# A fused attention, graph-convolution and LSTM block: ScalarE's reads and TensorE's products in a new order within each group of the first pass

## The chip, the cores and the metric

The kernel runs on one core of a Trainium2 chip. Five engines work side by side, each on its own queue in the order in which the program lists its instructions, and they hand work to each other through semaphores: TensorE (PE, with its weight loads shown as PEld), VectorE (DVE), ScalarE (ACT), GpSimd (POOL) and SyncE (SP), which issues the DMAs. A queue that waits holds up all that stands behind the wait. The metric is the device time of one execution in microseconds.

## The reference

`x` is 64 batches of 128 nodes of 128 features, `adj` a 128x128 graph. In short (biases and constants left out):

```
h   = relu(layernorm(x))                    # first norm
qkv = h @ W;  4 heads of 32                 # scores = q k^T / sqrt(32) + mask(adj)
x   = x + softmax(scores) @ v
h   = relu(layernorm(x))                    # second norm
h   = relu(adj @ (h @ Wg0 + bg0))           # first graph layer
h   = relu(adj @ (h @ Wg1 + bg1))           # second graph layer
for p in 1..4:                              # last state of an LSTM over windows of p nodes
    h[:, p-1::p] = lstm_last(p, h windows)
return x + h
```

Everything is float32; the products of the LSTMs and of q and k are made of three products of a value split into a high and a low part.

## The kernel before, in words

**Tiling.** The 64 batches are 16 groups of 4 batches, so that a group is one tile of 128 partitions x 512 columns, one PSUM bank. A first pass takes the groups through norm, attention, both graph layers and the LSTM of window 1. A second pass (the `walk` with its items, from about 314 us on) computes the LSTMs of windows 2 to 4 and stores the output; the change doesn't touch it.

**The first pass is a software pipeline.** `pipeline` (L455 on) calls `iteration(Step(k))` on each engine for k = 0 to 17: 0 and 1 are a fill of their own, 2 and 3 are written out, 4 to 13 are a hardware loop whose body holds two iterations, 14 to 17 are written out again, and 17 has a function of its own. In iteration k several groups are at work at different stages (the flags of `Step` say which stages exist):

- `front`: group k's q, k and v are projected and read, then the mask is put into the score banks (`put_mask`, L888) and the `scores` added (L883).
- `mid`: group k-1's softmax and attention: VectorE's two halves of `shift` (maximum L1170, difference L1172), ScalarE's `exp` (L599), the transposes of the probabilities (L776) and their reads (`read_probT`), `attend` (L867), `read_att` and `attended` (L776). POOL sums the exponentials (`add_halves`: L537, L539, L545).
- `back`: group k-2's `add_attention` (VectorE, L1188 and the add into X, L1193), second norm, `graph_mix` (L787), `graph_linear_1` (L805, L808), second `graph_mix`.
- `finish`: group k-3's `graph_linear_2` (L819, L824), `read_output` (ScalarE) and `output_lo` (VectorE, L1219), then the three gates of the window-1 LSTM, `first_gate` on TensorE (L839 to L841) and again on ScalarE (L608); `first_cell_part` on VectorE (L1200).
- `after`: group k-4's `first_h_part` (L1205) and `first_split` (L1211, L1213) on VectorE.
- `next1`, `next2`: the next groups' first norm (POOL, L527, and the moments on VectorE), transposes (L776) and reads (L644, L645).

**What sets the order.** The order of each engine is written by hand in its `iteration`. Several results share a PSUM bank, and so wait for each other: q, k and the attention's output in bank 4; the next group's transposes and the transposed attention in bank 5 (`psK`, `psR`); v, both mixes and the first linear in bank 6 (`psA`); the second linear and the three gates one after the other in bank 7 (`psB`); the scores and transposed probabilities in banks 0 to 3. On VectorE, `first_cell_part` stands ahead of `over_sums` and of the next iteration's `shift`, so the second gate's activation holds up the next iteration.

## Time and profile before

| | |
|---|---|
| median of 3 runs | 523.53 us (523.16 to 525.69) |
| the profiled execution | 523.03 us, its span 521.2 us |
| busy, of the span | PE 475.5 us (91%), DVE 427.9 (82%), ACT 350.4 (67%), POOL 223.2 (43%) |
| chain that ended last | PE 45%, DVE 32%, issue 10%, ACT 7%, POOL 2%, DMA 2% |

The profile is one execution, taken by the hardware profiler. The 1.8 us between 521.2 and 523.03 lie around the span. TensorE's busy time includes modelled ends of matmuls, so an engine that is 91% busy is not at 91% of its peak. The first pass takes the first 284 us or so; in the middle of it PE is about 94% busy and DVE about 90%. In the second pass PE is nearly always busy.

### The profile page before, as it was taken

The page shows a single profiled execution, that of the slowest core. Times are in us where ns is not written, and L with a number is a line of the kernel's source. Part 1 is how long each engine was busy: PE and PEld are TensorE (multiplying, and loading weights), DVE is VectorE, ACT ScalarE, POOL GpSimd, SP SyncE. Part 2 cuts the span into 40 slices and gives each one's busy share as a digit, 9 for nine tenths or more (in the row PEclk, how much of TensorE's full clock was granted, in tenths as well). Part 3 has the DMA queues.
Part 4 walks back from the last instruction along what each step waited for, and adds up shares of the span by engine and source line. Part 5 has one row for each costly group of instructions (what it writes and reads, how often), then busy time and mean ns, then how long its engine had stood idle before and what let it go on. Part 6 is the DMA issues. An engine that isn't in the chain of part 4 may idle for free.

```text
span 521.2 us, 10204 instructions
## 1 busy us (share of the span) xinstructions
PE 475.5 (91%) x3528; PEld 395.1 (76%) x3528; DVE 427.9 (82%) x929; ACT 350.4 (67%) x577; POOL 223.2 (43%) x229
## 2 busy tenths in 40 slices
PE   3767999999999999999979999999999999999994
PEld 2546878777777778777767777889999987888784
DVE  3958779889998899998985788888888889976775
ACT  2455777778777787777766777777766665665551
POOL 1476667776777667775442021221121222222211
PEclk9998999999999999999997999999999999999999
DMA  7323100000000000000000000000000000000225
GB/s 209 105 82 94 30 1 2 1 0 0 0 0 0 0 0 1 0 0 1 2 1 1 1 0 1 1 0 2 0 1 3 0 0 1 0 1 1 82 82 161
DMA packets 18779, 11.29 MB, mean 22 GB/s; under 512 B 662, under 2 KB 17724, under 8 KB 18748
## 3 DMA queue, kind: packets, MB, share of 16 engines
q1 hardware_dynamic: 17052, 10.03, 6.8%
q10 hardware_dynamic: 1696, 0.87, 0.6%
q8 instruction: 17, 0.28, 0.2%
q14 instruction: 14, 0.11, 0.1%
HBM read 6.70 MB, written 4.19 MB: 21 GB/s over the span
## 4 chain that ended last, share of the span: by engine, by line
PE 45%; DVE 32%; issue 10%; ACT 7%; POOL 2%; DMA 2%; DVEq 1%; SPq 0%; ACTq 0%; POOLq 0%
PE ps L934 25%; DVE rmax L1170 6%; PE ps L787 4%; PE ps L883 3%; DVE arena L1172 3%; DVE S_hi L1253 3%; PE ps L888 2%; DVE arena L1240 2%; DVE X L1193 2%; PE ps L839 2%; DVE stats L1097 2%; PE ps L776 2%; DMA X<-in_x_dram 2%; ACT arena L616 2%; ACT arena L608 2%
## 5 line engine op out<-in xcount | busy, mean ns | idle before, releaser
L630 ACT ACTIVATE arena<-ps,bias 128x512 f32<-128x512 f32 (+1 forms) x207 | 121.1, 624 | 47.0 <-PE ps L934 46.1
L594 ACT ACTIVATE arena<-ps 128x512 f32<-128x512 f32 (+1 forms) x128 | 89.9, 702 | 53.8 <-PE ps L787 28.8
L574 POOL TENSOR_TENSOR arena<-arena 128x512 f32<-128x512 f32 (+1 forms) x36 | 43.4, 1205 | 178.0 <-ACT arena L630 178.0
L934 PE MATMUL ps<-H_hi,W_hi 128*128 128x512 f32 (+2 forms) x207 | 75.6, 365 | 2.8 <-DVE S_lo L1255 2.0
L934 PE MATMUL ps<-H_lo,W_hi 128*128 128x512 f32 (+2 forms) x207 | 75.0, 362 | 0.0
L934 PE MATMUL ps<-H_hi,W_lo 128*128 128x512 f32 (+2 forms) x207 | 75.0, 362 | 0.0
L776 PE MATMUL ps<-ident,arena 128*128 128x128 f32 x448 | 60.7, 279 | 13.3 <-ACT arena L599 8.1
L776 PEld LDWEIGHTS ps<-ident,arena 128*128 128x128 f32 x448 | 52.1, 152 | 20.5 <-ACT arena L599 9.8
L537 POOL TENSOR_TENSOR arena<-arena 128x512 f32<-128x512 f32 x32 | 41.4, 1293 | 56.5 <-ACT arena L599 38.0
L519 POOL TENSOR_TENSOR rstd<-veps,minus_half 128x4 f32<-128x4 f32 x32 | 43.0, 1345 | 44.5 <-DVE veps L1105 44.5
L1240 DVE TENSOR_TENSOR arena<-arena 128x512 f32<-128x512 f32 (+1 forms) x53 | 34.0, 641 | 23.9 <-ACT arena L616 23.8
L934 PE MATMUL ps<-S_hi,W_lo 128*128 128x512 f32 (+1 forms) x144 | 51.9, 361 | 0.0
L934 PE MATMUL ps<-S_hi,W_hi 128*128 128x512 f32 (+1 forms) x144 | 51.8, 360 | 0.0
L934 PE MATMUL ps<-S_lo,W_hi 128*128 128x512 f32 (+1 forms) x144 | 51.7, 359 | 0.0
L616 ACT ACTIVATE arena<-arena 128x512 f32<-128x512 f32 (+1 forms) x57 | 32.3, 567 | 25.2 <-DVE arena L1233 25.1
L934 PEld LDWEIGHTS ps<-H_hi,W_hi 128*128 128x128 f32 x207 | 39.0, 188 | 9.5 <-DVE S_lo L1255 2.9
L527 POOL TENSOR_SCALAR arena<-X,mv,rstd 128x128 f32<-128x128 f32 x56 | 44.2, 801 | 1.5
L934 PEld LDWEIGHTS ps<-H_hi,W_lo 128*128 128x128 f32 x207 | 38.9, 188 | 5.5
L934 PEld LDWEIGHTS ps<-H_lo,W_hi 128*128 128x128 f32 x207 | 38.9, 188 | 5.0
L1170 DVE TENSOR_REDUCE rmax<-ps 128x8 f32<-128x1024 f32 x32 | 38.6, 1206 | 2.4 <-PE ps L883 1.3
L1172 DVE TENSOR_TENSOR arena<-ps,rmax 128x1024 f32<-128x1024 f32 x32 | 39.2, 1224 | 1.1
L787 PE MATMUL ps<-adjT,arena 128*128 128x128 f32 x256 | 38.0, 293 | 0.4 <-ACT arena L594 0.4
(107 smaller groups left out, 1001.2 us busy)
## 6 DMA issues: line engine op xcount, KB each, us to landing
X<-in_x_dram SPq DMA_DIRECT2D x16, 256.0 KB, 2.8
out_dram<-X SPq DMA_DIRECT2D x14, 256.0 KB, 2.4
out_dram<-X ACTq DMA_DIRECT2D x2, 256.0 KB, 3.9
arena<-in_L_gnn_W_dram ACTq DMA_DIRECT2D x1, 128.0 KB, 3.2
wg<-in_L_gnn_Wg_dram ACTq DMA_DIRECT2D x2, 64.0 KB, 2.3
bg_rows<-in_L_gnn_bg_dram SPq DMA_DIRECT2D x6, 0.5 KB
wv<-in_L_gnn_W_dram ACTq DMA_DIRECT2D x1, 64.0 KB, 3.2
adj_sb<-in_adj_dram SPq DMA_DIRECT2D x1, 64.0 KB, 3.4
```

The lines of the kernel that those rows point to most:

```text
L519: g_.tensor_tensor(rstd[:, layer, :], veps[:, layer, :], minus_half[:], ALU.pow).then_inc(done, 1)
L527: l = g_.tensor_scalar(xn[:, b, :], X[:, ds(g * GB + b, 1), :].rearrange("p a d -> p (a d)"), mv[:, 0, b, 0:1], rstd[:, 0, b:b + 1], ALU.s ...
L574: g_.tensor_tensor(ig[:, it.buf, 0:w], sig_i[:, it.buf, 0:w], tanh_g[:, it.buf, 0:w], ALU.mult)\
L594: a_.activation(to, psum, func).then_inc(ready, 1)
L616: a_.activation(tanh_c[:, it.buf, 0:width(it.p)], slot(cell, it), ACT.Tanh).then_inc(tanhs, 1)
L630: a_.activation(to[:, it.buf, 0:w], ps[:, 4 * it.par + j, 0:w], func, bias=bias[:, col:col + 1])\
L776: last = nc.tensor.transpose(to[:, b * P:(b + 1) * P], src[:, b, :], ident[:])
L787: l = mm(to[:, b, :], h[:, b * D:(b + 1) * D], adjT[:], start=True, stop=True)
L934: l = mm(o, wt, v, start=m == 0, stop=m == len(terms) - 1)
L1170: v_.tensor_reduce(rmax[:, part], s3[:, part, :], AX_X, ALU.max).then_inc(max_ready, 1)
L1172: v_.tensor_tensor(prob.rearrange("p (c n) -> p c n", n=N)[:, part, :], s3[:, part, :], rmax[:, part].unsqueeze(2).to_broadcast([P, 2 * GB ...
L1240: v_.tensor_tensor(h_f[:, it.buf, 0:w], sig_o[:, it.buf, 0:w], tanh_c[:, it.buf, 0:w], ALU.mult)\
```

## The change

Three engines get a new order within iterations 2 to 16. No instruction is added or removed.

- **ScalarE**: the second `exp` and both `read_probT` now stand ahead of the reads of k and v; the ReLU of the second norm (`hn2`) stands ahead of the reads of the next group (`read_hT`); `read_att` stands behind the first gate instead of behind the tanh; the third gate stands ahead of the read `u2T`.
- **TensorE**: the first gate stands between the two pairs of masks instead of ahead of all four; `attend` stands right behind `scores`; `attended` and the third gate stand ahead of the second mix.
- **VectorE**: `output_lo` stands ahead of `first_h_part`.

```diff
@@ ScalarE, iteration @@
                     read(qT[:], psQ, q_done, k + 1, q_ready)
                 if s.finish:
                     read_output(k - 3)
-                if s.front:
-                    read(kT[:], psQ, k_done, k + 1, k_ready)
-                    read_v(s)
                 if s.mid:
                     exp(s, 1)
                     read_probT(s, 0)
                     read_probT(s, 1)
+                if s.front:
+                    read(kT[:], psQ, k_done, k + 1, k_ready)
+                    read_v(s)
+                read(hn2, hn2, xn2_ready, k - 1, hn2_ready, ACT.Relu)
                 if s.next1:
                     read_hT(psX[s.back], k + 2, 1 - s.par)
-                read(hn2, hn2, xn2_ready, k - 1, hn2_ready, ACT.Relu)
...
                     first_gate(k - 3, 0, act_i, 0, 0.5)
+                if s.mid:
+                    read_att(s)
                 read(u1T[:], psA, u1_done, k - 1, u1T_ready)
...
-                if s.mid:
-                    read_att(s)
-                read(u2T[:], psA, u2_done, k - 1, u2T_ready)
                 if s.finish:
                     if s.after:
                         act.wait_ge(first_done, k - 3)
                     first_gate(k - 3, 2, act_o, 3, 0.5)
+                read(u2T[:], psA, u2_done, k - 1, u2T_ready)
@@ TensorE, iteration @@
                     transpose_prob(s, 1)
-                first_gate(s, 0, 0)
                 if s.front:
                     pe.wait_ge(probT_ready, k * 2 - 1)
                     put_mask((0, 1))
+                first_gate(s, 0, 0)
+                if s.front:
                     pe.wait_ge(probT_ready, k * 2)
                     put_mask((2, 3))
                     pe.wait_ge(k_ready, k + 1)
                     scores()
+                attend(s)
                 pe.wait_ge(hn2_ready, k - 1)
...
                 graph_linear_1().then_inc(z1_done, 1)
-                attend(s)
-                pe.wait_ge(h1_ready, k - 1)
-                interleave([], graph_mix(h1, u2_done, by_token_batch_first(psA)))
-                first_gate(s, 2, 3)
                 if s.next1:
                     pe.wait_ge(hT_hi_ready, k + 2)
                 attended(s)
+                first_gate(s, 2, 3)
+                pe.wait_ge(h1_ready, k - 1)
+                interleave([], graph_mix(h1, u2_done, by_token_batch_first(psA)))
@@ VectorE, iteration @@
                     add_attention(k)
+                if s.finish:
+                    output_lo(k - 3)
                 if s.after:
                     first_h_part(k - 4)
-                if s.finish:
-                    output_lo(k - 3)
```

TensorE's queue in the loop body of the kernel before, from the first gate (L839 to L841) to the end of the iteration; L888 are masks, L883 scores, L787 a mix, L805 and L808 the first linear, L867 `attend`, L776 the transposes of `attended`:

```order
L839 MATMUL ps<-H_hi,W_hi 128x512
...
L841 MATMUL ps<-H_hi,W_lo 128x512
L888 MATMUL ps<-mask,ident_bf 128x512 x4
L883 MATMUL ps<-arena 128x128 x16
L787 MATMUL ps<-adjT,arena 128x128 x4
...
L805 MATMUL ps<-bg_parts,sums_parts 128x512
L808 MATMUL ps<-wg,arena 128x128 x4
L867 MATMUL ps<-arena 32x128 x16
L787 MATMUL ps<-adjT,arena 128x128 x4
...
L776 MATMUL ps<-ident,arena 128x128 x4
```

The same stretch of the changed kernel, where the lines behind L832 are one higher (L840 to L842 the gate, L889 masks, L884 scores, L868 `attend`):

```order
L889 MATMUL ps<-mask,ident_bf 128x512 x2
L840 MATMUL ps<-H_hi,W_hi 128x512
...
L842 MATMUL ps<-H_hi,W_lo 128x512
L889 MATMUL ps<-mask,ident_bf 128x512 x2
L884 MATMUL ps<-arena 128x128 x16
L868 MATMUL ps<-arena 32x128 x16
L787 MATMUL ps<-adjT,arena 128x128 x4
...
L808 MATMUL ps<-wg,arena 128x128 x4
L776 MATMUL ps<-ident,arena 128x128 x4
...
L787 MATMUL ps<-adjT,arena 128x128 x4
```

Two masks moved ahead of the first gate; `attend` moved from behind the first linear to between scores and the first mix; `attended` and the third gate moved ahead of the second mix.

ScalarE's queue in the loop body before, from the read of the second linear (H_hi) to the first gate; L680 reads v, L599 is the second exponential, the x2 row is the two reads of the probabilities, L644 and L645 read the next group, and the last L594 row is the ReLU of the second norm:

```order
L594 ACTIVATE H_hi<-ps 128x512
L594 ACTIVATE arena<-ps 128x512
L679 REGISTER_ALU
L680 ACTIVATE arena<-ps 128x512
L599 ACTIVATE arena<-arena 128x1024
L594 ACTIVATE arena<-ps 128x1024 x2
L643 REGISTER_ALU
L644 ACTIVATE arena<-ps 128x512
L645 ACTIVATE S_hi<-ps 128x512
L594 ACTIVATE arena<-arena 128x512
L606 ISA
L608 ACTIVATE arena<-ps,half_bias 128x512
```

The same stretch of the changed kernel:

```order
L594 ACTIVATE H_hi<-ps 128x512
L599 ACTIVATE arena<-arena 128x1024
L594 ACTIVATE arena<-ps 128x1024 x2
L594 ACTIVATE arena<-ps 128x512
L679 REGISTER_ALU
L680 ACTIVATE arena<-ps 128x512
L594 ACTIVATE arena<-arena 128x512
L643 REGISTER_ALU
L644 ACTIVATE arena<-ps 128x512
L645 ACTIVATE S_hi<-ps 128x512
L606 ISA
L608 ACTIVATE arena<-ps,half_bias 128x512
```

The exponential and the reads of the probabilities moved ahead of k and v, and the ReLU ahead of the next group's reads.

## Rows read from the trace of the kernel before

**Rows 1.** Busy time by stretch: two successive iterations, k = 9 and 10.

```profile
core 0: us, PE busy (x) PEld busy (x) DVE busy (x) ACT busy (x) POOL busy (x), PEclk, DMA share, GB/s
150.20:166.85 16.65, 15.71 (x166) 12.50 (x158) 14.98 (x40) 12.76 (x21) 12.12 (x14) 1.00 0.00 0
166.85:182.95 16.10, 15.08 (x145) 12.21 (x145) 14.64 (x39) 12.12 (x20) 11.48 (x12) 1.00 0.00 0
```

**Rows 2.** Chain of waits through iteration 9: start us, us on the chain, what.

```profile
150.20 1.19 DVE rmax L1170
151.41 1.22 DVE arena L1172
...
158.36 0.11 DVE arena L1205
...
158.97 0.70 DVE H_lo L1219
...
159.80 0.49 PE ps L839
...
160.75 0.88 PE ps L888 x4
161.63 1.10 PE ps L883 x32
...
164.56 0.70 ACT arena L608
...
165.28 0.69 DVE arena L1200
```

**Rows 3.** Waits in 68.37 to 264.21, twelve iterations: total, times, longest.

```profile
DVE arena L1200 <- ACT arena L608: 7.4, 12, 2.1
PE ps L839 <- DVE H_lo L1219: 6.8, 12, 0.6
```

**Rows 4.** Chain of waits: attend as one piece, at full clock.

```profile
280.81 1.01 PE ps L867 x32
```

**Rows 5.** Timeline: u2T, first exponential, POOL's sums, add into X; iterations 9, 10, 15.

```profile
151.73 0.60 ACT L594 ACTIVATE arena<-ps 128x512 f32<-128x512 f32 x1 [0.46 <-PE ps L787]
153.01 1.04 ACT L599 ACTIVATE arena<-arena 128x1024 f32<-128x1024 f32 x1
155.50 0.73 POOL L539 TENSOR_TENSOR arena<-arena 128x256 f32<-128x256 f32 x1
155.80 0.97 DVE L1193 TENSOR_TENSOR X<-X,arena 128x512 f32 x1 [0.18 <-DVE arena L1188]
156.31 0.79 POOL L545 TENSOR_TENSOR arena<-arena 128x128 f32<-128x128 f32 x1
...
169.37 1.06 ACT L599 ACTIVATE arena<-arena 128x1024 f32<-128x1024 f32 x1
171.87 0.73 POOL L539 TENSOR_TENSOR arena<-arena 128x256 f32<-128x256 f32 x1
172.50 0.69 DVE L1193 TENSOR_TENSOR X<-X,arena 128x512 f32 x1 [0.17 <-DVE arena L1188]
...
253.52 1.19 DVE L1193 TENSOR_TENSOR X<-X,arena 128x512 f32<-128x512 f32 x1
```

**Rows 6.** Timeline of ScalarE, iteration 9: next group's read, ReLU, first gate.

```profile
160.14 0.59 ACT L644 ACTIVATE arena<-ps 128x512 f32<-128x512 f32 x1
...
161.13 0.63 ACT L594 ACTIVATE arena<-arena 128x512 f32<-128x512 f32 x1
161.67 0.67 ACT L608 ACTIVATE arena<-ps,half_bias 128x512 f32<-128x512 f32 x1
```

**Rows 7.** Timeline, iteration 3: VectorE's cell.

```profile
67.09 0.69 DVE L1200 SCALAR_TENSOR_TENSOR arena<-arena 128x512 f32<-128x512 f32 x1 [2.61 <-ACT arena L608]
```

**Rows 8.** Timeline, iteration 16: first gate, then VectorE waiting for the transposed attention.

```profile
273.60 0.80 PE L839 MATMUL ps<-H_hi,W_hi 128*128 128x512 f32 x1 [2.21 <-DVE H_lo L1219]
...
284.15 0.69 DVE L1188 TENSOR_TENSOR arena<-ps,rec 128x512 f32<-128x512 f32 x1 [2.32 <-PE ps L776]
```

**Rows 9.** Busy time by stretch: TensorE's granted clock inside iteration 16.

```profile
279.00:280.00 1.00, 1.00 (x6) 0.91 (x5) 0.00 (x0) 0.99 (x3) 0.00 (x0) 0.50 0.00 0
```

## The prediction, made before the changed kernel was run

> **What bounds the kernel now.** I read the busy time by slice first: the pass that the change touches is the first 284 us, and in the middle of it neither TensorE nor VectorE has much room. An iteration takes 16.65 or 16.10 us in turn, 16.4 on average, of which PE is busy 15.1 to 15.7 and DVE 14.6 to 15.0 [rows 1]. So about 0.7 to 1.5 us per iteration is waiting, and the reader should look for which waits lie on the chain. The chain of waits answers that. Through iteration 9 it runs down VectorE from the first maximum (150.20) to the low part of the output, L1219 (158.97); then over to TensorE for the first gate at 159.80, four masks, scores, first mix and second gate; then ScalarE's gate at 164.56 and VectorE's cell at 165.28, behind which the next iteration's maximum is queued [rows 2]. The table of waits confirms both hand-overs: the first gate waited for L1219 in each of twelve iterations, 6.8 us in all, and the cell waited for ScalarE's gate in each, 7.4 us, of which one is 2.1 and the others about 0.48 [rows 3]. It is one loop: 9.6 us of VectorE, 5.5 us of TensorE and ScalarE (159.80 to 165.28), and the rest VectorE again. Its length is the period, and anything not on it is hidden.
>
> **What the change does to this loop, iterations 4 to 15.**
>
> *Output_lo first.* L1219 takes the slot of L1205, which starts at 158.36 against 158.97 [rows 2]: the first gate can start 0.61 us earlier. The pair together is as long as before, so VectorE's own queue loses nothing.
>
> *Two masks ahead of the gate.* Four masks take 0.88 us on the chain [rows 2]. Two of them now run while TensorE would wait for L1219 anyway: 0.44 us off the chain.
>
> *Attend ahead of the first mix.* Its 32 pieces take 1.01 us [rows 4], and they now stand between scores and the mix, on the chain. Before, they stood behind the first linear, off it. So +1.01.
>
> The three together: -0.61 - 0.44 + 1.01 = -0.04 us per iteration, -0.5 us over twelve. The three moves on TensorE and VectorE nearly cancel: attend eats what the others free.
>
> *ScalarE's new path to the second gate.* The ReLU starts when the norm is done (161.13), and the first gate's activation followed 0.54 us behind. Now the two reads of the next group stand between them; they took 0.99 us together (160.14 to 161.13) [rows 6]. The first gate's activation moves to about 162.66 and ends at 163.33, and TensorE's second gate, which uses the same bank, can't start before. On the other path ScalarE's second gate starts at 164.56 - 0.04, and a gate's three products take 0.95 us (159.80 to 160.75), so TensorE's starts at about 163.55. So ScalarE has about 0.2 us of slack: no cost, but little room.
>
> *Reads of k and v later.* The scores wait for k. In the old order the second read of the probabilities was over at 160.14, where the next group's read began [rows 6]; with k behind it that gives 160.14 + 0.6 = 160.7, against scores that could start at 161.63 - 0.61 - 0.44 = 160.6. So at worst 0.1 us per iteration. It is less, since the second exponential, ahead of the probability reads, no longer stands behind two reads of 0.6 us each and the whole train comes earlier. I take nothing.
>
> *Third gate and attended ahead of the second mix, and what that does on GpSimd.* This is where I see the largest term. In iteration 9 the first exponential started at 153.01, though its input was ready at 151.41 + 1.22 = 152.63: ScalarE was still busy with the third gate, the last thing in its order. In iteration 10 it started 2.52 us behind the first maximum, that is at once [rows 1, 2, 5]. Behind it, GpSimd's L537, L539, L545 follow in a fixed train, and VectorE's add into X lands in this train. In iteration 10 L539 ends at 172.60, the add starts at 172.50 and takes 0.69. In iteration 9 L539 ends at 156.23, the add starts at 155.80 and takes 0.97 [rows 5]. The add seems to wait for the GpSimd instruction that runs when it comes, less 0.15. Now u2T comes last. It started at 151.73 [rows 5], and TensorE has attended and a gate ahead of its mix (I estimate 1.1 to 1.4 us, the gate 0.95 at most) in place of attend (1.01), so it ends at 152.4 to 152.7, and I let the exponential start at 152.65, 0.36 earlier; L539 ends at 155.87 and the add takes 0.69, as in iteration 10. Worth 0.28 us on the chain in each of the five odd iterations 5 to 13: -1.4 us. The iterations outside the loop have the same late exponential and longer adds: 0.87 in iteration 4, 1.07, 1.19 and 1.17 in 14, 15 and 16 (the longest: [rows 5]); by the same shift they lose 0.17, 0.37, 0.40 and 0.38: -1.3 us. Together -2.7. The even iterations of the loop gain nothing.
> The Trainium skill (SBUF — State Buffer, "SBUF: two separate sides") says that a VectorE instruction with two SBUF inputs and a GpSimd instruction that reads SBUF exclude each other for the whole instruction, whichever starts first. By that the add would cost 0.43 + 0.69 = 1.12 in iteration 9, where the trace shows 0.97, and the sum would be 0.7 us larger. The trace agrees with the kind of the effect and not quite with its size.
>
> **The ends of the pass.**
>
> *Iterations 2 and 3.* There is no first_h_part yet, so L1219 gains nothing, and in iteration 3 VectorE waited 2.61 us for the second gate, until 67.09 [rows 7]: this chain is TensorE's and ScalarE's alone. Scores start about where they did, 0.1 us sooner, attend adds 1.01 us ahead of the mix, and the cell moves to about 68.0: +0.9 us, and nothing gives it back. Bounds: 0 if ScalarE's earlier exponential moves scores a full microsecond, 1.3 if iteration 2 is late too.
>
> *Iteration 16.* No scores here. TensorE stood idle 2.2 us before the first gate at 273.60 and then ran at half clock [rows 8, 9]; attend stood behind the first linear, and add_attention of the last iteration waited until 284.15 for it, 2.32 us [rows 8]. Now attend fills the gap between first gate and first mix, and attended comes before the third gate. At half clock (0.50, the 1.2 GHz level) attend takes up to 2.0 us in a gap of about 1 us (the gate's 0.61 and what the mix waited), so part of it pushes the mix, but its 1.01 us behind the first linear goes, and so does the 2.32 us wait of L1188, which can start about 2 us earlier. The work behind is TensorE's own (two items of the second pass) and absorbs half of that. I take -1.1 us, between 0 and -2.3.
>
> **Sum.** -0.5 - 2.7 + 0.9 - 1.1 = -3.4 us. The profiled execution took 523.03, so 519.6 by its own measure; the median of the runs is 0.5 higher (523.53), and on that scale I predict 520.1 us. About 0.5% (2.6 us) is what a measurement can tell from no change, so this is a small gain just beyond it.
>
> **Rivals.**
>
> *A. The add into X doesn't get shorter* (the exponential stays where it is, because u2T now stands last on ScalarE and waits for a mix that comes later). For it: the read of u2T moved behind the third gate, and I leave it only 0.2 us ahead of the exponential. Against it: 0.2 us too little would delay the exponential by that alone, half of what it gains. Then the sum is -0.5 + 0.9 - 1.1 = -0.7: 522.8 us, no change that can be told. 32%.
>
> *B. The loop gets shorter by the whole wait of the cell.* If scores or attend overlap better than their pieces suggest, the cell waits no more, and VectorE alone sets the period. That is worth up to 0.45 us more for each of twelve iterations, at most 5 us: 515 to 518. For it: DVE is busy less than 15 us. Against it: attend and scores have never run back to back in this order, and nothing shows a gain. 12%.
>
> *C. Slower: the train on GpSimd comes too early.* The margin works against the add as well. L545 follows L539 by 0.81 us (156.31 against 155.50) [rows 5]; in the new order it starts at 155.95, only 0.15 behind the add's start. If the train is 0.2 us earlier or the add 0.2 later, the add meets L545 instead and waits for nearly all of its 0.79: 1.3 us instead of 0.97 or 0.69, that is +0.35 in odd and +0.6 in even iterations. From 0.15 us on it decides. Twelve times 0.5 is +5.7, with the other terms (-0.7) +5: 528. A half of it, in one parity, gives 525. In the same way ScalarE's 0.2 us of slack to the second gate could be used up, at 0.2 per iteration. 12% for this side.
>
> *D. The change does nothing to the loop and its ends cancel*: 523. It is within A's result.
>
> **From the cases to the numbers.** Forecast 44%, A and D 32%, B 12%, C 12%. The forecast's own spread is 518.5 to 521.5, and its upper part falls within 0.5%. So faster by over 0.5%: most of the forecast's 44% and B, 0.52. Within 0.5%: 0.37. Slower by over 0.5% only in C: 0.11. The range 517.3 to 523.8 takes in forecast and A, and leaves the far ends of B and C out.
>
> **What would show each step.** In the changed profile: first gate's wait for L1219 near zero or at the same 0.5 but 0.6 earlier behind the first maximum (8.7 to 9.0 us instead of 9.6); first exponential 2.45 to 2.5 us behind the first maximum in odd iterations too; the adds into X all near 0.70; the cell's wait for ScalarE still 0.3 to 0.5 in each iteration; periods near 16.3 and 16.05; the first maximum of iteration 4 about 0.9 later than 68.37; the last iteration's L1188 nearer to 282. The prediction is wrong if the adds keep their length, if the reads of k hold up the scores, or if the ReLU's place on ScalarE makes the second gate late.

## The result and the profile after

The changed kernel takes 520.52 us (median of 10 runs, 518.19 to 521.48) against 523.51 for the kernel before (10 runs, 522.56 to 525.69): a ratio of 0.9925, 95% interval 0.9903 to 0.9947. The forecast was 520.1. A second series of six runs gave 518.67 against a kernel before at 524.36 in that series (0.9907, 0.9882 to 0.9931). So the kernel became faster, by 0.5 to 1.2%.

The page of the profiled execution (519.47 us, span 517.7), busy time by engine and the chain that ended last:

```profile
PE 472.9 (91%) x3528; PEld 393.5 (76%) x3528; DVE 424.3 (82%) x929; ACT 350.7 (68%) x577; POOL 221.7 (43%) x229
...
PE 47%; DVE 31%; ACT 9%; issue 8%; DMA 2%; POOL 1%; DVEq 1%; SPq 0%; ACTq 0%; POOLq 0%
```

VectorE's busy time fell by 3.6 us though it runs the same instructions: 2.6 of these are the shorter adds into X (14.1 us in all before, 11.5 after), and the rest isn't taken apart here. Where the 3.5 us of span went is read best from the start of each group's first maximum, taken from VectorE's timeline. Two executions of each kernel stand side by side, in us:

| stretch | before | before, again | after | after, again |
|---|---|---|---|---|
| span's start to first maximum of k = 2 | 36.96 | 37.29 | 38.25 | 37.24 |
| k = 2 to k = 4 | 31.41 | 31.24 | 32.45 | 32.48 |
| k = 4 to k = 16 (twelve iterations) | 195.84 | 195.93 | 193.50 | 193.59 |
| k = 16 to the add into X in iteration 17 | 20.67 | 20.89 | 16.71 | 16.69 |
| from there to the end | 236.32 | 236.35 | 236.79 | 236.78 |

The first row is not the change's: between 20 and 30 us TensorE's granted clock was 0.83 in the profiled execution after and 1.00 in the one before, and the second execution after starts 1.0 us earlier. drain_only below, which has the first two iterations as before the change, showed 0.83 there too and reached this maximum at 38.27. The other rows repeat to 0.2 us. The change costs 1.0 us in iterations 2 and 3, gives 2.3 in the twelve and 4.0 around iteration 16, and 0.5 of that is lost behind it.

**Inside the twelve iterations.** Busy time by stretch of the changed kernel, k = 9 and 10 (columns as in [rows 1]):

```profile
151.76:168.14 16.38, 15.63 (x152) 12.51 (x151) 14.64 (x40) 12.83 (x21) 12.17 (x14) 1.00 0.00 0
168.14:184.25 16.11, 14.94 (x149) 11.92 (x148) 14.58 (x38) 12.15 (x20) 11.48 (x12) 1.00 0.00 0
```

The odd iteration went from 16.65 to 16.38, the even one stayed at 16.1 [rows 1]. The chain of waits through iteration 9, which answers to [rows 2]:

```profile
151.76 1.19 DVE rmax L1172
...
157.36 0.70 DVE X L1195
...
159.67 0.70 DVE H_lo L1221
...
160.50 0.49 PE ps L840
...
161.46 0.45 PE ps L889 x2
161.91 1.10 PE ps L884 x32
163.01 1.01 PE ps L868 x32
164.02 1.09 PE ps L787 x8
...
165.84 0.70 ACT arena L608
...
166.56 0.69 DVE arena L1202
```

Measured from the first maximum, the first gate starts at 8.74 us (160.50 - 151.76) and was at 9.60: 0.86 earlier, which is about the swap's 0.61 and the shorter add's 0.28. From the gate to the cell it is 6.06 us and was 5.48 (159.80 to 165.28 in [rows 2]): +0.58, which is attend's 1.01 less two masks. The cell is therefore at 14.80 instead of 15.08, and that 0.28 is the whole gain of the iteration. The reader should see L868 standing on the chain: before, attend wasn't on it.

Waits of the same twelve iterations (70.70 to 264.20), which answer to [rows 3]:

```profile
DVE arena L1202 <- ACT arena L608: 11.9, 12, 2.5
...
PE ps L840 <- DVE H_lo L1221: 2.1, 10, 0.2
```

The gate's wait for the low part shrank from 6.8 to 2.1, and the cell's wait for ScalarE grew from 7.4 to 11.9. VectorE reaches the cell earlier than before and waits longer there. Timeline of iteration 9 for the exponential, GpSimd's train and the norm, which answers to [rows 5]:

```profile
154.23 1.06 ACT L599 ACTIVATE arena<-arena 128x1024 f32<-128x1024 f32 x1 [0.39 <-DVE arena L1174]
...
156.73 0.73 POOL L539 TENSOR_TENSOR arena<-arena 128x256 f32<-128x256 f32 x1
157.36 0.69 DVE L1195 TENSOR_TENSOR X<-X,arena 128x512 f32 x1 [0.18 <-DVE arena L1190]
157.54 0.83 POOL L545 TENSOR_TENSOR arena<-arena 128x128 f32<-128x128 f32 x1
...
159.67 0.69 DVE L1221 SCALAR_TENSOR_TENSOR H_lo<-ps,H_hi 128x512 f32 x1
159.79 1.03 POOL L519 TENSOR_TENSOR rstd<-veps,minus_half 128x4 f32<-128x4 f32 x1 [1.41 <-DVE veps L1107]
160.28 0.68 DVE L1207 SCALAR_TENSOR_TENSOR arena<-arena 128x512 f32<-128x512 f32 x1
160.88 1.11 DVE L1112 TENSOR_SCALAR arena<-X,mv,rstd 128x128 f32 x4
```

The exponential starts 2.47 us behind the maximum (2.81 before) and now waits for its input, the add takes 0.69 in each of the loop's ten iterations (0.79 in 14 and 15). The last four lines hold what I had not seen coming: GpSimd's `rstd` takes 1.03 us and the normalization L1112 waits for nothing. The same place in the kernel before:

```profile
158.36 0.69 DVE L1205 SCALAR_TENSOR_TENSOR arena<-arena 128x512 f32<-128x512 f32 x1
158.51 1.43 POOL L519 TENSOR_TENSOR rstd<-veps,minus_half 128x4 f32<-128x4 f32 x1 [1.42 <-DVE veps L1105]
...
159.98 0.34 DVE L1110 TENSOR_SCALAR arena<-X,mv,rstd 128x128 f32 x1 [0.32 <-POOL rstd L519]
```

There `rstd` met first_h_part, which reads two operands from SBUF, and took 0.40 us more; VectorE then waited 0.32 for it in each of the twelve iterations. With output_lo first, whose one operand is in PSUM, both are gone.

**Iteration 3 and iteration 16.** Timeline of VectorE after, the cell of iteration 3, which answers to [rows 7]:

```profile
69.42 0.69 DVE L1202 SCALAR_TENSOR_TENSOR arena<-arena 128x512 f32<-128x512 f32 x1 [2.12 <-ACT arena L608]
```

Timeline of iteration 16 after, which answers to [rows 8]:

```profile
272.60 0.50 PE L840 MATMUL ps<-H_hi,W_hi 128*128 128x512 f32 x1 [1.35 <-DVE H_lo L1221]
...
273.50 1.08 PE L868 MATMUL ps<-arena 128*32 128x128 f32 x32
...
274.92 1.16 PE L787 MATMUL ps<-adjT,arena 128*128 128x128 f32 x8 [0.34 <-ACT arena L594]
...
280.18 0.69 DVE L1190 TENSOR_TENSOR arena<-ps,rec 128x512 f32<-128x512 f32 x1
```

Attend fills the gap between the gate and the mix, and add_attention (L1190) no longer waits for TensorE: it starts 15.98 us behind the first maximum of k = 16 (19.94 before). TensorE's granted clock is 1.00 here, the 2.4 GHz level, through the whole stretch; before it was 0.50, the 1.2 GHz level, in part of it [rows 9]. Busy time by stretch of the changed kernel, 262 to 282 us:

```profile
262.00:282.00 20.00, 15.12 (x122) 12.09 (x122) 15.99 (x36) 14.62 (x23) 6.73 (x7) 1.00 0.00 1
```

The same stretch before had a mean granted clock of 0.83, in both of its executions.

### The profile page after: what moved, and what is told of

Read it like the earlier page. It is cut to its first block, busy times and chain, and to the rows that moved or that the text cites. A ratio compares the mean times of both kernels' runs of the same rounds, so it can differ in the third digit from the quotient of the medians.

```text
span 517.7 us, 10204 instructions
## 1 busy us (share of the span) xinstructions
PE 472.9 (91%) x3528; PEld 393.5 (76%) x3528; DVE 424.3 (82%) x929; ACT 350.7 (68%) x577; POOL 221.7 (43%) x229
## 4 chain that ended last, share of the span: by engine, by line
PE 47%; DVE 31%; ACT 9%; issue 8%; DMA 2%; POOL 1%; DVEq 1%; SPq 0%; ACTq 0%; POOLq 0%
PE ps L935 26%; DVE rmax L1172 6%; PE ps L787 4%; DVE arena L1174 3%; PE ps L884 3%; PE ps L868 3%; DVE S_hi L1255 3%; PE ps L776 3%; DVE arena L1242 2%; ACT arena L608 2%; DMA X<-in_x_dram 2%; DVE arena L1202 2%; ACT arena L594 2%; ACT arena L616 2%; PE ps L840 2%
## 5 line engine op out<-in xcount | busy, mean ns | idle before, releaser
L594 ACT ACTIVATE arena<-ps 128x512 f32<-128x512 f32 (+1 forms) x128 | 88.4, 703 | 46.0 <-PE ps L776 20.0
L776 PE MATMUL ps<-ident,arena 128*128 128x128 f32 x448 | 58.3, 280 | 8.6 <-ACT arena L599 3.3
L537 POOL TENSOR_TENSOR arena<-arena 128x512 f32<-128x512 f32 x32 | 41.5, 1297 | 56.4 <-ACT arena L599 37.7
L776 PEld LDWEIGHTS ps<-ident,arena 128*128 128x128 f32 x448 | 52.6, 154 | 10.4 <-issue 2.9
L519 POOL TENSOR_TENSOR rstd<-veps,minus_half 128x4 f32<-128x4 f32 x32 | 37.9, 1185 | 42.1 <-DVE veps L1107 42.1
L527 POOL TENSOR_SCALAR arena<-X,mv,rstd 128x128 f32<-128x128 f32 x56 | 48.2, 874 | 1.5
L599 ACT ACTIVATE arena<-arena 128x1024 f32<-128x1024 f32 x32 | 33.9, 1059 | 15.9 <-DVE arena L1174 15.9
```

The lines of the kernel that those rows point to most:

```text
L519: g_.tensor_tensor(rstd[:, layer, :], veps[:, layer, :], minus_half[:], ALU.pow).then_inc(done, 1)
L527: l = g_.tensor_scalar(xn[:, b, :], X[:, ds(g * GB + b, 1), :].rearrange("p a d -> p (a d)"), mv[:, 0, b, 0:1], rstd[:, 0, b:b + 1], ALU.s ...
L537: g_.tensor_tensor(by_64, pv[:, :, 0:N // 2], pv[:, :, N // 2:N], ALU.add).then_inc(by_64_ready, 1)
L594: a_.activation(to, psum, func).then_inc(ready, 1)
L776: last = nc.tensor.transpose(to[:, b * P:(b + 1) * P], src[:, b, :], ident[:])
```

## The experiments

Each kernel was timed against the kernel before on the same chip, and each ratio is to that series' own median of the kernel before (523.19 to 524.36); before_again is a single execution. The stretches in the last three columns come from one profiled execution of each kernel. "Loop" is the time from the first maximum of k = 4 to that of k = 16.

| kernel | median us | ratio, 95% interval | loop | k = 2 to 4 | k = 16 to add of 17 |
|---|---|---|---|---|---|
| before | 523.51 | | 195.84 | 31.41 | 20.67 |
| after | 520.52 | 0.9925 (0.9903, 0.9947) | 193.50 | 32.45 | 16.71 |
| dve_old | 526.99 | 1.0073 (1.0046, 1.0100) | 200.56 | 32.45 | 18.14 |
| tail_old | 520.51 | 0.9942 (0.9918, 0.9967) | 193.89 | 32.44 | 16.86 |
| pool_waits | 519.79 | 0.9934 (0.9913, 0.9954) | 193.34 | 31.56 | 19.62 |
| drain_only | 522.46 | 0.9978 (0.9956, 0.9999) | 195.82 | 31.24 | 18.83 |
| loop_only | 521.52 | 0.9951 (0.9934, 0.9969) | 193.59 | 32.44 | 19.17 |
| fill_old | 518.72 | 0.9894 (0.9866, 0.9921) | 193.54 | 31.20 | 17.82 |
| attend_only | 534.50 | 1.0200 (1.0176, 1.0224) | 206.05 | 33.23 | 18.79 |
| attend_late | 511.24 | 0.9763 (0.9734, 0.9793) | 186.20 | 31.19 | 18.09 |
| attend_late_gate | 508.02 | 0.9693 (0.9663, 0.9722) | 183.47 | 30.68 | 18.09 |
| all_moves | 507.79 | 0.9687 (0.9657, 0.9716) | 182.77 | 30.64 | 16.62 |

**dve_old: the changed kernel with VectorE's old order.**

```diff
                 if s.back:
                     add_attention(k)
+                if s.after:
+                    first_h_part(k - 4)
                 if s.finish:
                     output_lo(k - 3)
-                if s.after:
-                    first_h_part(k - 4)
```

> The changed kernel with VectorE's old order alone (first_h_part ahead of output_lo). Theory: output_lo is on the loop, since the first gate waits for it, so the cell comes 0.6 us later in each of twelve iterations: +7 us on the changed kernel, about 527.5, and slower than the kernel before (523.5). Rival: TensorE's own train (value, transposes, masks) now decides when the first gate starts, for the changed profile shows it waiting only 0.2 us for L1221: then little changes, 520.5 to 522. First gate's wait for the low part: 0.8 us by the theory and by the rival too, but by the rival the period stays 16.25.

Slower than before by 0.7%. The loop is 7.06 us longer than the changed kernel's, 0.59 per iteration, and the adds are still 0.69: the swap's term of 0.61 holds. Its timeline in iteration 9:

```profile
161.57 0.69 DVE L1207 SCALAR_TENSOR_TENSOR arena<-arena 128x512 f32<-128x512 f32 x1
161.72 1.43 POOL L519 TENSOR_TENSOR rstd<-veps,minus_half 128x4 f32<-128x4 f32 x1 [1.41 <-DVE veps L1107]
...
163.01 0.49 PE L840 MATMUL ps<-H_hi,W_hi 128*128 x1 [0.78 <-DVE H_lo L1221]
163.19 0.60 DVE L1112 TENSOR_SCALAR arena<-X,mv,rstd 128x128 f32 x2 [0.32 <-POOL rstd L519]
```

`rstd` is back at 1.43 and the normalization's wait at 0.32. It is the order of these two VectorE instructions, and nothing else in the change, that shortened `rstd`.

**tail_old: the changed kernel with the third gate behind the second mix again, on TensorE and ScalarE.**

```diff
@@ ScalarE @@
+                read(u2T[:], psA, u2_done, k - 1, u2T_ready)
                 if s.finish:
                     if s.after:
                         act.wait_ge(first_done, k - 3)
                     first_gate(k - 3, 2, act_o, 3, 0.5)
-                read(u2T[:], psA, u2_done, k - 1, u2T_ready)
@@ TensorE @@
                 attended(s)
-                first_gate(s, 2, 3)
                 pe.wait_ge(h1_ready, k - 1)
                 interleave([], graph_mix(h1, u2_done, by_token_batch_first(psA)))
+                first_gate(s, 2, 3)
```

> The changed kernel with the third gate behind the second mix again, on TensorE and ScalarE. Theory of the prediction: the third gate's place ahead of the mix is what frees ScalarE for the first exponential, so the adds into X go back from 0.69 to about 0.97 in odd iterations and the time to 523. Rival: that attend left the stretch behind the first linear (1.0 us) is enough; the exponential still starts 2.45 us behind the first maximum, the adds stay at 0.69, and the time is within 0.5 us of the changed kernel's (520.5).

No difference from the changed kernel that the runs can tell (the intervals overlap), and 0.39 us more in the loop. ScalarE's timeline in iteration 9, whose first maximum is at 151.33:

```profile
152.62 0.60 ACT L594 ACTIVATE arena<-ps 128x512 f32<-128x512 f32 x1 [0.73 <-PE ps L787]
153.32 0.69 ACT L608 ACTIVATE arena<-ps,half_bias 128x512 f32<-128x512 f32 x1
153.91 1.05 ACT L599 ACTIVATE arena<-arena 128x1024 f32<-128x1024 f32 x1
```

The exponential still stands behind the third gate, as before the change, and yet starts 2.58 us behind the maximum and not 2.81; the add takes 0.73 and not 0.97. So 0.24 of the 0.28 comes from something else: attend is no longer ahead of the second mix, so mix, gate and exponential all come earlier. (attend_only below moves nothing but attend, and has the same 0.73, with the exponential 2.57 behind.) The prediction gave this to the third gate's place, and that was wrong; the gate's place is worth 0.04 in iteration 9 (and 0.16 in iteration 15).

**pool_waits: the kernel before, in which GpSimd's second addition (L539) waits for the add into X.**

```diff
                 pool.wait_ge(by_64_ready, n)
+                if half == 0 and s.back:
+                    pool.wait_ge(x2_ready, s.k - 1)
```

> The kernel before, with one wait added: in the first half GpSimd's second sum (L539) waits until VectorE's add into X is done, so that no GpSimd instruction reads SBUF while the add runs. Theory: the add then takes 0.69 us in all iterations, 0.28 to 0.5 less in nine of them, on the chain, -2.7 us: 520.8. GpSimd has 2 us to spare there and the reciprocal root is not late. Rival: the length of the add is no term of the loop, or the waiting train makes the root late: 523.5 or more, with normalize's wait for GpSimd above 0.32.

Timeline in iteration 9 (L541 is the second addition here, L1195 the add into X):

```profile
155.21 0.69 DVE L1195 TENSOR_TENSOR X<-X,arena 128x512 f32 x1 [0.18 <-DVE arena L1190]
156.05 0.74 POOL L541 TENSOR_TENSOR arena<-arena 128x256 f32<-128x256 f32 x1 [1.21 <-DVE X L1195]
```

All adds take 0.69. Those of k = 4 to 15 took 10.76 us before (twelve rows of VectorE's timeline) and take 8.28, 2.48 less, and the loop is 2.50 shorter. Nothing but this wait was added, and the exponential is as late as before (2.82 behind the maximum). So every tenth that the add met on GpSimd stood on the chain, and in the loop this one wait gives as much as the whole change does (2.50 us against 2.34). That the ratios are alike too, 0.9934 against 0.9925, leans on the end of the pass: behind k = 16 this execution is 1.05 us shorter, 0.48 of it the add's (1.17 to 0.69), and TensorE's clock over that stretch was 0.91 and not 0.83.

**drain_only and loop_only: which part of the gain is iteration 16's.** drain_only is the kernel before with TensorE's and ScalarE's new order in iteration 16 alone; loop_only is the changed kernel with their old order there.

```diff
@@ drain_only, TensorE @@
                 first_gate(s, 0, 0)
+                if s.at == GROUPS:
+                    attend(s)
...
-                attend(s)
+                if s.at == GROUPS:
+                    attended(s)
+                    first_gate(s, 2, 3)
+                else:
+                    attend(s)
...
```

> The kernel before with the new order of attend, attended and third gate in iteration 16 alone. Theory: what the prediction gave to the end of the pass and to the clock: add_attention of iteration 17 starts 2 to 4 us earlier; -1.1 us if TensorE still falls to half clock there, -3 if it keeps the full clock because attend fills the gap: 520.5 to 522.4. Rival: TensorE's work behind absorbs it all: 523.5.

> The changed kernel with the old order of attend, attended, third gate and second mix in iteration 16 alone. Theory: what iteration 16 gives is a term by itself, -1.2 us in the mean as in the kernel with the new order there alone; here it is lost: 521.7, with 20 us or so from the first maximum of iteration 16 to the add into X of iteration 17 instead of 16.7 to 18.8. Rival: the 3.96 us that the profile shows there come from the clock only and come in any kernel: then the median is 520.5.

drain_only gains 1.2 us by its medians (523.68 to 522.46) and 1.84 by the stretch behind k = 16, over which its clock was 0.91, with half clock for about 3.5 us of it. loop_only leaves the loop as it was (193.59), and its stretch is 19.17 instead of 16.7; by the ratios it is 0.26 and 0.44% (1.4 and 2.3 us) behind the two series of the changed kernel; its interval overlaps the first one's and not the second's. So iteration 16 is worth about 1 to 2.5 us.

**fill_old: the changed kernel with attend, attended and read_att in their old places in iterations 2 and 3.**

```diff
-                attend(s)
+                if s.at > 3:
+                    attend(s)
                 pe.wait_ge(hn2_ready, k - 1)
...
```

The lines left out do the same for attended (TensorE) and read_att (ScalarE).

> The changed kernel with attend, attended and read_att back in their old places in iterations 2 and 3 alone. Theory: attend ahead of the first mix costs these two iterations 1.0 us, since no first_h_part is there whose place output_lo could take: 1.0 us less than the changed kernel, 519.5, with 31.4 us from the first maximum of iteration 2 to that of iteration 4 instead of 32.45. Rival: the loss comes from ScalarE's new order, which makes the low part of the next group late (iteration 2's length 14.57 against 13.74); then the distance stays near 32.3 and the time at 520.5.

k = 2 to 4 takes 31.20 us, 1.25 less. Iteration 2 alone is as long as after the change (14.57, before 13.74), so its 0.83 isn't attend's. There are no gates in iteration 2 yet, and VectorE has no output_lo there, so of the change only ScalarE's order is left for it. VectorE's timeline shows where it lands, before and after:

```profile
48.99 0.73 DVE L1117 TENSOR_TENSOR S_lo<-arena,S_hi 128x512 fp32r<-128x512 f32 x1 [0.56 <-ACT S_hi L645]
...
51.60 0.69 DVE L1119 TENSOR_TENSOR S_lo<-arena,S_hi 128x512 fp32r<-128x512 f32 x1 [1.88 <-ACT S_hi L645]
```

The next group's low part S_lo waits for ScalarE's read L645, which now stands behind the reads of k and v and the ReLU: it starts 12.70 us behind the first maximum (50.95 - 38.25) instead of 11.40 (48.36 - 36.96), and VectorE waits 1.3 us longer. Part of that is won back in a wait for GpSimd that is gone.

Iteration 3 alone is 16.63 (after 17.88, before 17.67), although its add into X now takes 1.36. So attend, with attended and its read, costs iteration 3 about 1.25, somewhat more than attend's 1.01, and the change's other moves give iteration 3 1.04 back. Theory and rival of the expectation each held for one of the two iterations. Its 0.9894 lies below the changed kernel's ratio, as the 1.2 us ask, but the intervals overlap.

**attend_only: the kernel before with attend right behind the scores, and nothing else.**

```diff
                     scores()
+                attend(s)
                 pe.wait_ge(hn2_ready, k - 1)
...
                 graph_linear_1().then_inc(z1_done, 1)
-                attend(s)
                 pe.wait_ge(h1_ready, k - 1)
```

> The kernel before with one move: attend right behind scores on TensorE, all else old. Theory: 1.01 us on the path from the low part to the cell in each of twelve iterations, and the same in iteration 3, +13; less 2.5 to 3 because u2T and the third gate come 1 us sooner, the first exponential is early and the adds into X take 0.69 us; less 1 at the end of the pass: 531 to 534. Rival: attend hides behind something in this kernel too, and only the gains are left: 520.

Slower by 2.0%, 10 us (534.50, just above the range that I expected). Its waits in the twelve iterations:

```profile
DVE arena L1200 <- ACT arena L608: 19.5, 12, 3.1
```

7.4 became 19.5, that is 1.01 us more in each iteration, exactly attend's duration [rows 4]. The periods are 17.10 and about 17.45 (16.10 and 16.65 before): +1.00 in the even ones, +0.8 in the odd ones, where the add falls to 0.73. The other moves must pay for all this before the change gains anything.

**attend_late: the changed kernel with attend behind the first linear in iterations 2 to 15, but ahead of the third gate and the second mix; attended stands behind that mix and read_att behind the tanh again.** The gates and masks, ScalarE's order of exponential and ReLU, and VectorE's swap stay.

```diff
                     scores()
-                attend(s)
+                if s.at == GROUPS:
+                    attend(s)
...
                 graph_linear_1().then_inc(z1_done, 1)
-                if s.next1:
-                    pe.wait_ge(hT_hi_ready, k + 2)
-                attended(s)
+                if s.at == GROUPS:
+                    attended(s)
+                else:
+                    attend(s)
                 first_gate(s, 2, 3)
                 pe.wait_ge(h1_ready, k - 1)
                 interleave([], graph_mix(h1, u2_done, by_token_batch_first(psA)))
+                if s.at != GROUPS:
+                    if s.next1:
+                        pe.wait_ge(hT_hi_ready, k + 2)
+                    attended(s)
...
```

> The changed kernel with attend behind the first linear again in iterations 2 to 15, followed by the third gate, the second mix and attended; ScalarE reads the attention behind the tanh; iteration 16 as in the changed kernel. Theory: attend's 1.01 us leaves the path from the low part to the cell, and ScalarE's path (ReLU, two reads, first gate) is next, 0.2 us shorter, so the cell comes 0.2 us sooner in each of twelve iterations; but the third gate's activation and u2T come 1 us later, the first exponential with them, and the adds into X meet GpSimd for 0.3 to 0.4 us. The two nearly cancel in the loop; without the loss of iterations 2 and 3: 519 to 520. Rival: attend costs nothing where it stands and the time rises by the contention alone, 523 to 524.

511.24 us: 2.4% under the kernel before, and my expectation of it fell. The later exponential that I expected didn't come (it starts 2.47 us behind the maximum, the adds take 0.69), and I had set the floor of this kernel too high, because I had left out that the normalization starts earlier. Its chain through iteration 9, from the ReLU on:

```profile
156.59 0.04 ACT arena L594
...
157.13 0.58 ACT arena L644
157.71 0.49 ACT S_hi L645
158.20 0.59 ACT arena L608
...
158.83 0.50 PE ps L842
...
159.83 0.70 ACT arena L608
160.55 0.69 DVE arena L1210
```

The cell is at 14.21 behind the first maximum (160.55 - 146.34) instead of 14.80. Attend's 1.01 is off the chain, and 0.59 of it is gained, because another path takes over: TensorE's second gate (158.83) now waits for ScalarE's first gate (158.20), which stands behind the reads L644 and L645 of the next group. That is the path whose slack the prediction put at 0.2 us; in the profile after it is 0.67 (first gate on ScalarE over at 164.20, second gate on TensorE at 164.87), and it is the bound once attend is gone. 0.59 twelve times is 7.1, the loop is 7.30 shorter. The cell still waits for ScalarE here, 4.6 us in the twelve iterations instead of 11.9.

**attend_late_gate: attend_late with ScalarE's first gate right behind the ReLU.**

```diff
                 read(hn2, hn2, xn2_ready, k - 1, hn2_ready, ACT.Relu)
-                if s.next1:
-                    read_hT(psX[s.back], k + 2, 1 - s.par)
                 if s.finish:
                     if s.after:
                         act.wait_ge(first_h, k - 3)
                     first_gate(k - 3, 0, act_i, 0, 0.5)
+                if s.next1:
+                    read_hT(psX[s.back], k + 2, 1 - s.par)
```

> As the kernel with attend late, and on ScalarE the first gate stands right behind the ReLU, ahead of the next group's two reads. Theory: ScalarE's path gets 1 us shorter too, so VectorE no longer waits for the second gate (0.8 us per iteration in the changed kernel) and its own queue sets the period: 0.4 to 0.8 us less per iteration, less 0.3 where the adds meet GpSimd: 514 to 518. Rival: TensorE's train ahead of the first gate is the next bound and keeps the period at 16: 519.

508.02 us, again below what I expected (514 to 518). The loop is 2.73 us shorter again. Its chain through the same iteration has no TensorE and no ScalarE left; the last pieces:

```profile
159.02 0.94 DVE S_lo L1127
159.96 0.60 DVE arena L1210
...
161.44 1.24 DVE rmax L1180
```

The cell follows VectorE's own S_lo at once; it waited for ScalarE in two of the twelve iterations, 1.7 us in all. The adds are met by GpSimd again (0.74 to 0.78 in odd iterations, 0.91 and 1.12 in 14 and 15).

**all_moves: attend_late_gate with GpSimd's wait of pool_waits.**

> As attend_late_gate, with GpSimd's second sum of the first half waiting for the add into X as well. Theory: the adds take 0.69 us everywhere and VectorE sets the period, near 15.5 us: 510 to 514. Rival: the same time as attend_late_gate, if the adds don't matter any more once VectorE is the bound; this can't be if VectorE's queue sets the period, so it would speak for TensorE.

507.79 us, 0.9687 (0.9657 to 0.9716), below the 510 to 514 that I expected: 3.1% under the kernel before and, by the ratios, 2.2 to 2.4% under the changed one. Against attend_late_gate the medians tell nothing; the loop is 0.70 us shorter and all adds of the loop are 0.69. Busy time by stretch, k = 9 and 10:

```profile
143.83:159.28 15.45, 15.36 (x162) 12.46 (x151) 14.56 (x40) 12.62 (x20) 11.36 (x13) 1.00 0.00 0
159.28:174.51 15.23, 14.89 (x148) 12.27 (x149) 14.51 (x39) 12.26 (x20) 10.72 (x13) 1.00 0.00 0
```

PE waits 0.1 us in the odd iteration and 0.3 in the even one, where it waited 0.9 and 1.0 in [rows 1]; DVE waits 0.9 and 0.7 (1.7 and 1.5 before).

**after_again and before_again: both kernels unchanged, the second in one execution.**

> The changed kernel itself again, for its time beside the others and for a second trace. If TensorE's clock in 272 to 282 is chance, this trace can show 0.66 to 0.83 there in place of 1.00, and the stretch from the first maximum of iteration 16 to the add of iteration 17 is then 18 us or more instead of 16.7; if the full clock is the new order's doing, it shows 1.00 again. The periods are 16.09 and 16.39 again.

> The kernel before itself again, one look. The same question from the other side: if the clock in 272 to 282 is chance, it needn't be 0.66 here. The adds are 0.69 and 0.97 in turn again.

The table at the top holds both. The loop and iterations 2 and 3 repeat within 0.2 us; the late start of the profiled execution does not; the clock of iteration 16 does (0.83 before and 1.00 after, each time).

## Why the prediction was right, point by point

The time and the side were right: 520.1 forecast, 520.52 and 518.67 measured. That they came out so close is in part luck, as the terms show. The terms, against the stretches:

| term | forecast | measured |
|---|---|---|
| swap, masks and attend, twelve iterations | -0.5 | -0.1 |
| add into X, k = 4 to 15 | -2.3 | -2.3 |
| add into X, k = 16 | -0.4 | -0.4, inside the stretch below |
| iterations 2 and 3 | +0.9 | +1.0 (+1.2 in the second pair) |
| iteration 16 without its add | -1.1 | -3.6 in the stretch, and +0.5 given back behind it |

Forecast they add up to -3.4, measured to -4.9. The profiled pair differs by 3.5 only because the execution after lost 1.3 us before its first maximum of k = 2 (38.25 against 36.96); the spans of the second pair (521.7 and 516.8) differ by 4.9. So the gain was forecast 1.5 us too small: iteration 16 gave 2.0 more than its term, and the rest 0.5 less. The median of 520.52 doesn't show that.

**The near-cancelling was right.** First gate 0.86 earlier, path behind it 0.58 longer. dve_old gives the swap as 0.59 per iteration, attend_only gives attend as 1.01. No run moves the masks alone; dve_old's loop is 5.5 us shorter than attend_only's, 0.4 of it in the adds, which leaves 0.43 per iteration for the masks, the third gate's place and ScalarE's order together, against the 0.44 forecast for the masks. The shortfall of 0.4 us over twelve iterations is below what single starts tell.

**The adds were right in size, in the main wrong in cause.** Each add is at 0.69 and each tenth counts (pool_waits: 2.48 against 2.50). But the step "u2T comes last, so the exponential is free earlier" was only the smaller part: tail_old puts the gate back and keeps 0.24 of the 0.28. I had seen that attend stood ahead of the second mix in the kernel before, and set against it attended and a gate, which are about as long together; with the gate in its old place only attended is left there (tail_old), or nothing (attend_only), and the mix comes earlier by that.

**The wait of the cell.** I forecast 0.3 to 0.5 per iteration; the iterations of the loop have about 0.8, and the twelve together 11.9 us. Here a step was missing: I took VectorE's side as fixed but for the swap and the add, and didn't see that `rstd` had been lengthened by first_h_part and would be 0.40 shorter. VectorE gained 0.3 us more than I counted, and since the other path was the later one, all of it went into waiting. It cost the forecast nothing, but it hid what was to be had. Rival B (the cell waits no more, 515 to 518) didn't come with this change; with attend late the wait falls from 11.9 to 4.6 us and the time is 511, and in attend_late_gate it is all but gone (1.7 us) and the time is 508. That is lower than B's figure: B priced the wait at 0.45 per iteration, and it was about 0.8, because VectorE's side is shorter than I had it; and these kernels also save 1.3 to 1.8 us in iterations 2 and 3.

**Iterations 2 and 3: the sum right, its parts wrong.** I put +0.9 into iteration 3 and said that nothing gives it back. Measured are +0.83 in iteration 2, which I had only in the upper bound, and +0.21 in iteration 3 (+0.41 in the second pair), where attend costs what it should (fill_old) and the other moves repay most of it. What I had put at nothing in iteration 2 is ScalarE's order: the read that S_lo waits for comes 1.3 us later. Two errors of about 0.8 us cancelled, and that is luck.

**Reads of k and v.** I took nothing, and in iteration 9 the scores start right behind the masks (161.91, where the two masks at 161.46 end), so k holds nothing up there.

**ScalarE's path.** I said 0.2 us of slack and no cost. No cost was right, and the slack is 0.67, since the norm comes earlier. It is the first thing that binds when attend leaves (attend_late).

**Iteration 16.** I forecast -1.1 within 0 and -2.3, and the stretch is 4.0 shorter with the add. The wait of add_attention went, as described. What I had not counted is that the clock would stay at 1.00: my term assumed half clock. In the executions whose clock was 0.90 or 0.91 over the stretch itself, it takes 19.17 and 19.62 in the old order (loop_only, pool_waits) and 17.82, 18.09 and 18.09 in the new one (fill_old, attend_late, attend_late_gate); drain_only, whose add is 1.19 long, takes 18.83. So at like clock the order gives 1.1 to 1.8, my term or somewhat more; with the add's 0.4 taken off too, 1.8 to 2.5 us of the 4.0 are left, which I put down to the clock, 0.83 before and 1.00 after. That the sum stayed in range although this was left out is luck. Which clock comes is not set by the order of iteration 16 alone. fill_old has exactly the changed kernel's iteration 16, and its stretch reads:

```profile
262.00:282.00 20.00, 15.47 (x116) 12.06 (x115) 15.86 (x38) 13.88 (x21) 6.73 (x7) 0.91 0.00 1
```

TensorE had waited 1.34 us for the low part ahead of the first gate there, and 1.35 in the changed kernel, so the length of this wait doesn't decide it. What does stays open.

**Rivals.** A (the adds stay) fell at once, and D with it. C (the train meets the add at L545) didn't come: L545 starts 0.18 us behind the add in iteration 9, as close as foreseen, and the add, having started first, took 0.69.

## What to carry to other kernels

When a reordering moves a piece from a place with slack onto the loop that sets the period, price it there alone before adding the gains of the other moves: attend's 1.01 us per iteration ate what the swap and the masks freed, and moving it back out (attend_late, 0.9763) brought 1.5 to 1.6% on the changed kernel, more than the 0.75 to 0.93% of the whole change. A wait that grows after a change (the cell's, 7.4 to 11.9) shows where the gain is stored and which path to shorten next. And where an instruction's duration varies between iterations, look at what runs beside it and let one of the two wait: one semaphore wait on an engine with time to spare gave as much in the loop as the new order of three engines.

## What the runs showed of the hardware

In these traces a VectorE instruction with two SBUF operands and a GpSimd instruction hold each other up, in both directions. The add into X waits for a running L539 (0.97 us in place of 0.69, with 0.43 of L539 left); and GpSimd's small `rstd` (128x4) waits for a running first_h_part. In both, the extra time is what is left of the other instruction less 0.14 to 0.15 us: `rstd` started at 158.51, first_h_part ended at 159.05, the remainder is 0.54 and `rstd` was 0.40 longer. The largest case is iteration 3 of fill_old: the add starts at 58.10 with 0.81 of L537 left (57.63 to 58.91) and takes 1.36, 0.67 more. output_lo, with one operand in PSUM, lengthened nothing: `rstd` ran beside it in 1.03 us.

The Trainium skill (SBUF — State Buffer, "SBUF: two separate sides") has this as a lock that either engine holds for its whole instruction. The trace agrees on the kind of operands and on both directions. It disagrees on "the whole instruction": in iteration 9 after, first_h_part starts at 160.28, in the middle of `rstd` (159.79 to 160.82), and takes 0.68 us, with nothing added, where the rule would add 0.54. The measurement decides: this GpSimd instruction of 128x4 values can block VectorE for at most the first 0.49 of its 1.03 us. What it does in that first part no run shows, and the profile's spans on GpSimd are rough.

Two executions of the changed kernel differ by 1.0 us in the first 38 us (first maximum at 38.25 and 37.24), with a granted clock between 24 and 30 us of 0.72 in the one and 1.00 in the other. Its ten runs go from 518.19 us (mean granted clock 0.993) to 521.48 (0.985): the spread from run to run, which goes with the clock, is as large as the change itself.
